# Cross-attention and mixture-of-experts block on one core: turning the attention output in 32x32 blocks on VectorE instead of on TensorE, with the low parts of x, context and attention output on GpSimd

## The reference

```python
x = x + xattn(layernorm(x), ctx)         # 16 heads of 16, softmax over 128 context tokens, then wo and its bias
x = x + ffn(layernorm(x))                # top-1 of 8 experts; LayerNorm again inside, scale/bias per expert,
                                         # 256 -> 64, exact gelu, 64 -> 256, only the chosen expert's row is kept
```

## Time and profile before

| what | value |
|---|---|
| time, median of 3 runs | 1593.97 us (1592.43 to 1604.42) |
| the profiled execution's own time | 1596.52 us |
| its span (first to last instruction) | 1594.5 us |
| busy PE / DVE / ACT / POOL | 94% / 75% / 56% / 27% of the span |
| attention | the first 1056 us or so |
| chain of work that ended last | PE 89%, DVE 5%, issue 3%, ACT 2% |

### The profile page before, as it was taken

How to read it: one execution, slowest core, us unless ns; L and a number is a source line. 1 busy time by engine, 2 the same in 40 slices (tenths; PEclk the granted TensorE clock), 3 DMA queues, 4 the chain that set the end, 5 groups by cost and what they waited for, 6 DMA issues and landing times.

```text
span 1594.5 us, 39584 instructions
## 1 busy us (share of the span) xinstructions
PE 1506.3 (94%) x15438; PEld 1210.1 (76%) x15438; DVE 1188.9 (75%) x2880; ACT 891.7 (56%) x1450; POOL 424.2 (27%) x600
## 2 busy tenths in 40 slices
PE   6899999999999999999999999879999999999998
PEld 5677777777778777878877787757777777777776
DVE  4787788767887788778777877667777777777775
ACT  4567666666667667767776777543342423333332
POOL 3223222222223223222322232112323232222221
PEclk9999999999999999999999999999999999999999
DMA  7466545554566556645654665402221212121221
GB/s 185 120 174 164 156 126 154 150 152 135 141 161 160 153 137 162 170 135 154 162 155 133 157 167 145 117 30 70 66 68 54 80 54 80 54 80 54 70 64 40
DMA packets 150480, 190.89 MB, mean 120 GB/s; under 512 B 17631, under 2 KB 101146, under 8 KB 150298
## 3 DMA queue, kind: packets, MB, share of 16 engines
q1 hardware_dynamic: 150298, 188.38, 43.1%
HBM read 53.01 MB, written 33.55 MB: 54 GB/s over the span
## 4 chain that ended last, share of the span: by engine, by line
PE 89%; DVE 5%; issue 3%; ACT 2%; DMA 1%; SPq 0%; ACTq 0%
PE s_ps L1195 12%; PE st_ps L1213 12%; PE pp_ps L1075 11%; PE pv_ps L1023 9%; PE s_ps L980 8%; PE pp_ps L1048 7%; PE st_ps L1008 7%; PE pp_ps L1083 5%; PE pp_ps L1069 4%; PE pv_ps L1031 3%; PE t_ps L999 3%; DVE negmax L729 2%; PE pp_ps L1161 2%; PE s_ps L1202 2%; ACT pT L636 1%
## 5 line engine op out<-in xcount | busy, mean ns | idle before, releaser
L729 DVE TENSOR_REDUCE negmax<-s_ps 128x8 f32<-128x1024 f32 x256 | 312.4, 1221 | 90.7 <-PE s_ps L980 83.4
L585 ACT ACTIVATE pT<-st_ps 128x1024 f32<-128x1024 f32 x256 | 262.7, 1026 | 101.9 <-PE st_ps L1008 101.8
L1213 PE MATMUL st_ps<-w_hi,q_packed 128*128 128x256 f32 x1024 | 213.2, 294 | 0.7 <-DVE q_packed L840 0.7
L1195 PE MATMUL s_ps<-k_packed,w_hi 128*128 128x512 f32 x512 | 172.8, 419 | 18.4 <-ACT pT L636 18.4
L1023 PE MATMUL pv_ps<-pT,v 128*32 128x128 f32 x4096 | 166.5, 278 | 24.8 <-DVE attn L742 12.5
L456 POOL TENSOR_TENSOR q_parts<-q,q_parts 128x1024 bf16<-128x1024 f32 x32 | 68.3, 2134 | 446.0 <-ACT q_parts L579 446.0
L980 PE MATMUL s_ps<-k_packed,q_packed 96*128 96x128 bf16 x2048 | 158.7, 221 | 18.4 <-issue 13.7
L1213 PEld LDWEIGHTS st_ps<-w_hi,q_packed 128*128 128x128 f32 x1024 | 168.4, 189 | 9.8 <-issue 6.4
L628 ACT ACTIVATE offhotT<-pv_ps 96x512 bf16<-96x512 bf16 x31 | 18.4, 592 | 253.1 <-PE pv_ps L1182 253.1
L1008 PE MATMUL st_ps<-q_packed,k_packed 98*128 98x128 bf16 x2048 | 158.9, 221 | 0.2 <-DMA q_packed<-negmaxT 0.2
L980 PEld LDWEIGHTS s_ps<-k_packed,q_packed 96*128 96x128 bf16 x2048 | 124.1, 98 | 44.3 <-issue 29.0
(11 more groups left out here) (179 smaller groups left out, 3511.7 us busy)
## 6 DMA issues: line engine op xcount, KB each, us to landing
q_packed<-q_parts SPq DMA_DIRECT2D x192, 256.0 KB, 3.8
k_packed<-k_parts SPq DMA_DIRECT2D x192, 256.0 KB, 4.4
xin<-in_x_dram SPq DMA_DIRECT2D x32, 512.0 KB, 3.8
cin<-in_ctx_dram SPq DMA_DIRECT2D x32, 512.0 KB, 3.9
x_scratch<-xb SPq DMA_DIRECT2D x32, 512.0 KB, 4.3
xin<-x_scratch SPq DMA_DIRECT2D x32, 512.0 KB, 4.6
out_dram<-xb SPq DMA_DIRECT2D x32, 512.0 KB, 3.2
q_packed<-negmaxT SPq DMA_DIRECT2D x128, 8.0 KB
```

What stands on the lines that cost most here:

```text
L585: a.activation(pT[u % 2][:], st_ps[:], ACT.Exp, scale=DH ** -0.5).then_inc(s_exp, 1)
L729: v.tensor_reduce(own, s_ps[:].rearrange("p (h s) -> p h s", s=P), AX_X, ALU.max, negate=True).then_inc(s_red, 1)
L1195: t.matmul(h_ps[m % 2], w[:, c, e, :].bitcast(F32R), x[n % 2][:, c, :].bitcast(F32R), start=(k == 0 and c == 0), stop=False)
L1213: t.matmul(o, h[n % 2][:, m, tok].bitcast(F32R), w[:, m, :].bitcast(F32R), start=(m == 0 and k == 0), stop=False)
```

## The change

DVE has an instruction that transposes each 32x32 block of its input by itself. As every head fills exactly 32 rows of `pv_ps`, one such instruction turns the bank into a tile with queries on the partitions, and a second one turns the divided result back for the projection. The order of features that this leaves is made good by a permuted order of wo's columns and v's bias. In detail:

- PE: `turn_pv` and `turn_attn` go; `values` of a new sequence waits for DVE's first turn (it waited for the division); `turn_max` waits for nothing of the attention output any more. Items 2 to 5 no longer wait for the low parts but for ACT; items 4 and 5 wait for the low parts of x, 6 and 7 for those of the context.
- ACT: `keep_pvT` goes; for items 0 to 3 it copies the bank a second time, in full precision, to the SBUF tile `turned[k % 2]`, once POOL has read what was there before. `keep_attn` reads SBUF.
- DVE: `turn_values` (a 128x512 transpose from PSUM) comes first in odd units, ahead of `maxima`; `norm` now ends with a 128x256 transpose in SBUF, which waits until ACT and POOL have read the sequence before; `rest_of_attn` and `lower` go.
- POOL: it takes `rest_of_attn` (128x256) and `lower` (128x512, from `turned`). Its group is no longer three calls but an order by pairs of units, and `residual` is cut in two halves.
- Start: POOL copies wo into the new order ahead of its first `norm`, once wo has been loaded; v's bias is loaded with two DMAs in runs of 16 numbers. The one-hot tiles of the expert layer lie in the same memory as `turned`.

```diff
@@ gpsimd
+            pool.wait_ge(s_w[3], 16)
+            for co in range(C):
+                for c in range(C):
+                    g.tensor_copy(wo_dense[:, co, c * P:(c + 1) * P].rearrange("p (s f d) -> p s f d", s=STRIPS, f=2),
+                                  dense(w_in[3][:, co, :])[:, c]).then_inc(s_wd, 1)
...
+            def rest_of_attn(n, b):
+                pool.wait_ge(s_ath, at(GB, n, b + 1))
+                hi, lo = aT[b % 2]
+                g.tensor_tensor(lo[:].bitcast(F32R), attnT[:], hi[:], ALU.subtract).then_inc(s_ate, 1)
+            def lower(n, k):
+                hi, lo = (xT, cT)[k // 2]
+                pool.wait_ge(s_pe, at(ITEMS, n, k + 1))
+                g.tensor_tensor(lo[:, k % 2, :].bitcast(F32R), turned[k % 2], hi[:, k % 2, :],
+                                ALU.subtract).then_inc(s_tl, 1)
...
-            def group(n):
-                if n < LAST:
-                    lo(n + 1, 0)
-                if n + 2 <= LAST:
-                    norm(n + 2)
-                if n < LAST:
-                    lo(n + 1, 1)
-                    residual(n + 1)
+            def group(n):
+                for u in range(0, UNITS, 2):
+                    if turned_at(n, u):
+                        rest_of_attn(*turned_at(n, u))
+                    if u == 0 and n < LAST:
+                        lo(n + 1, 0)
+                    if u == 2 and n + 2 <= LAST:
+                        norm(n + 2)
+                    if u == 2 and n < LAST:
+                        lo(n + 1, 1)
+                    if u == 4 and n + 2 <= LAST:
+                        lower(n + 2, 0)
+                    if u == 4 and n < LAST:
+                        residual(n + 1, 0)
+                    if u == 4 and n + 2 <= LAST:
+                        lower(n + 2, 1)
+                        lower(n + 2, 2)
+                    if u == 4 and n < LAST:
+                        residual(n + 1, 1)
+                    if u == 6 and n + 2 <= LAST:
+                        lower(n + 2, 3)
@@ scalar
-            def keep_pvT(n, b):
-                act.wait_ge(s_pv, at(UNITS, n, C * (b + 1)))
-                wait(act, s_tpv, at(GB, n, b))
-                a.copy(uvT[:], pv_ps[:]).then_inc(s_uv, 1)
...
-                    last = a.copy((xT, cT)[k // 2][0][:, k % 2, :].bitcast(F32R), ps[:])
+                    a.copy((xT, cT)[k // 2][0][:, k % 2, :].bitcast(F32R), ps[:]).then_inc(s_full, 1)
+                    wait(act, s_tl, at(4, n, k - 1))
+                    last = a.copy(turned[k % 2], ps[:])
@@ vector
+            def turn_values(n, b):
+                dve.wait_ge(s_pv, at(UNITS, n, C * (b + 1)))
+                wait(dve, s_nrm, at(GB, n, b))
+                v.transpose(pv_by_q[:], pv_ps[:]).then_inc(s_tpv, 1)
             def norm(n, b):
                 dve.wait_ge(s_tpv, at(GB, n, b + 1))
                 v.reciprocal(recip[:], pv[:, :, DH]).then_inc(s_rc, 1)
...
+                dve.wait_ge(s_nrm, at(GB, n, b + 1))
+                wait(dve, s_ath, at(GB, n, b))
+                wait(dve, s_ate, at(GB, n, b))
+                v.transpose(attnT[:].rearrange("p c t -> p (c t)"), attn[:]).then_inc(s_at, 1)
@@ tensor
                 if m == 0:
-                    wait(pe, s_nrm, at(GB, n, b))
+                    wait(pe, s_tpv, at(GB, n, b))
...
-            def turn_pv(n, b):
-                pe.wait_ge(s_uv, at(GB, n, b + 1))
-                for k in range(4):
-                    mm = t.transpose(pv_ps[:, k * P:(k + 1) * P], uvT[:, k * P:(k + 1) * P], ident[:])
-                mm.then_inc(s_tpv, 1)
...
-                if 2 <= k < 6:
-                    pe.wait_ge(s_tl, at(4, n, k - 1))
+                if 4 <= k < 8:
+                    pe.wait_ge(s_tl, at(4, n, 2 * (k // 2 - 1)))
```

More of the change, by code:

```diff
@@ L117, in xattn_moe @@
         v1 = [sb(f"v{n}", [P, GB, H, HP]) for n in range(2)]
+        shared = sb("shared", [P, 2, GT])
+        turned = [shared[:, n, :] for n in range(2)]
         xb = [sb(f"xb{n}", [P, GB, D]) for n in range(2)]
@@ L456, in lo, with residual @@
                 g.tensor_tensor(parts[z][:, 2, :, :], z32[z][:], parts[z][:, 1, :, :], ALU.subtract).then_inc(s_lo, 1)
[L458 to L463, removed]
+            def rest_of_attn(n, b):
[7 more added lines that the diff above has]
+                                ALU.subtract).then_inc(s_tl, 1)
+            def residual(n, half):
+                if half == 0:
+                    pool.wait_ge(s_xn, at(GB, n, GB))
+                    wait(pool, st_x2[n % 2], (n // 2) * 16)
+                for b in range(2 * half, 2 * half + 2):
                     last = g.tensor_tensor(xb[n % 2][:, b, :], xin[n % 2][:, b, :], bo_all[:], ALU.add)
-                last.then_inc(s_xb, 1)
+                if half == 1:
+                    last.then_inc(s_xb, 1)
             norm(0)
+            for k in range(4):
+                lower(0, k)
             g.memset(v1[0][:, :, :, DH:HP], 1.0).then_inc(s_vone, 1)
@@ L472, in _ @@
             g.memset(v1[1][:, :, :, DH:HP], 1.0).then_inc(s_vone, 1)
+            for k in range(4):
+                lower(1, k)
             pool.wait_ge(s_bo, 1)
-            residual(0)
+            for half in range(2):
+                residual(0, half)
             for e in range(E):
@@ L513, in lo_of_xT @@
                                 ALU.subtract).then_inc(f_xl, 1)
-            ffn_norm(0)
-            ffn_norm(1)
+            def group(n):
[19 more added lines that the diff above has]
+                        lower(n + 2, 3)
+                    if u == 2 and n == LAST:
+                        ffn_norm(0)
+                    if u == 4 and n == LAST:
+                        ffn_norm(1)
+            for n in range(GROUPS):
+                group(n)
             lo_of_xT(0)
+            rest_of_attn(LAST, GB - 2)
+            rest_of_attn(LAST, GB - 1)
             def ffn_group(n):
@@ L874, in _ @@
             v.tensor_copy(bo_all[:], t_ps[:, 0:D]).then_inc(s_bo, 1)
-            for k in range(3):
-                lower(1, k)
             dve.wait_ge(s_c1T, 1)
@@ L883, in _ @@
             last.then_inc(s_c1, 1)
-            lower(1, 3)
             remainder(1, 4)
@@ L900, in group @@
                         remainder(n + 2, 4)
-                    if more2 and u == 6:
-                        rest_of_attn(*done)
-                        lower(n + 2, 3)
-                    if more2 and u == 5:
-                        norm(*done)
+                    if done and u % 2 == 1:
+                        turn_values(*done)
                     if later(n, u, 3):
                         maxima(*later(n, u, 3))
-                    if done and u % 2 == 1 and not (more2 and u == 5):
+                    if done and u % 2 == 1:
                         norm(*done)
@@ L1236, in odd @@
             def odd(n, u):
-                ahead, nxt, done = later(n, u, 3), later(n, u, 1), turned_at(n, u)
+                ahead = later(n, u, 3)
                 if ahead:
```

97 lines of the change are left out of this document (34 added, 63 removed).

## The result

| kernel | median | runs |
|---|---|---|
| before | 1593.31 us | 1592.43 to 1604.42 (4) |
| after | 1655.71 us | 1654.19 to 1658.76 (4) |

The ratio is 1.0377 (95% interval 1.0329 to 1.0426): slower by 62 us, where 1586 was forecast and 1636 was the upper end of the range. The profiled execution has a span of 1654.4 us.

The account below looks back on a forecast made before the run. PE looked like the bound, but SP queue, POOL and DVE end the three stretches: 7.0 + 8.9 + 15.0 = 30.9 against 31.1 us, -6; start +4, end -6: -8, profiled 1588.5, median 1586 us; range 1548 to 1636.

Parts of the forecast that it names:

- four maxima at 1.56: DVE's four maxima in units 7, 0, 1 and 2, counted as 6.24 us of its 14.5 us sum.
- units 7, 0, 1 and 2: Stretch of a group, 15.60 us before: DVE will be last, 15.0 us after, gain 0.6 us.
- Units 3 and 4: Stretch of 7.18 us before: PE waits for the SP queue's last pack of k until about 7.0, gain 0.2 us.
- Units 5 and 6: Stretch of 8.32 us before: PE waits for POOL's low part of the attention output, 8.9 us, loss 0.6 us.
- Rival D: POOL is slowed by its neighbour DVE, one 0.42 us case a group in units 5 and 6: +12, 1598; chance 0.08.
- the transposes: DVE's new turns in odd units: 0.69 us for 128x512 and 0.41 for 128x256, 4.4 us a group.
- The start: Start of the kernel: POOL copies wo first, PE's first item moves from 13.01 to about 16.6: +4, between 0 and 8.
- The end: Last two groups: PE waits for the first turn alone, no longer for the division: -6, between -8 and 0.
- Rival A: In each group POOL and the pack do not hold PE; 29.3 us a group, about 1545 in all; chance 0.22.
- Rival B, the clock: Waits at unit 5 and in unit 6 lower the clock; half the groups lose about 1.7 us: +26, 1612; chance 0.15.
- a sign of being wrong: The forecast is wrong if the clock column falls below 0.97 in the steady windows.
- Rival C, slow turning: DVE's turns take their upper bounds, 1.6 us a group more in units 7 to 2: +50, 1636; chance 0.15.

Follow-up runs that it names:

- without the reads: The two small DVE instructions of the maxima made memsets that read nothing, in both kernels: after 1573.49 us, before 1579.19 us.
- with one input each: Kernel after, with the two small DVE instructions of the maxima replaced by three reductions that each read one SBUF tile: 1610.18 us, ratio 1.0089.
- the turning alone: Kernel before plus only the two DVE turns replacing PE's and ACT's copy; low parts stay on DVE, POOL keeps its old list: 1691.89 us, ratio 1.059.
- experiment 1: Both kernels with the small maxima instructions as memsets, maxima not subtracted from the scores: after 1573.49 us (ratio 0.9871), before 1579.19 us (0.9897).

## Why the prediction was wrong

By its own steps:

- **"four maxima at 1.56 (1.22 and two small ones, each after the one before)": the term that failed.** It stands in the sum for units 7, 0, 1 and 2, where DVE was rightly held to be last, and it priced L783 and L785 at their time in before. One of the eight there met POOL's `lo` of q in every group and waited for it, 1.83 us a group. The stretch was forecast at 15.0 and took 17.31 us in the mean. That it is this term: without the reads the stretch is 14.41, or 15.3 with the shorter `memset`s made good (eight times 0.106); with one input each it is 15.76, or 15.0 less the third instruction's four times 0.2. Some 0.2 to 0.5 us of the 17.31 is left to other causes, the clock among them.
- **The rest of the walk held.** Units 3 and 4: 7.71 against 7.77 before, a gain of 0.1 where 0.2 was forecast. (The 7.0 of the prediction is for the one group that it walked, which was shorter than the mean.) In the group shown above they took 8.35 us (676.80 to 685.15), with the last pack of k issued 2.52 us behind unit 3 as forecast. In the trace it landed at 685.06, 5.74 us later, where 4.4 were counted; such late landings are in before too (mean 4.85 us in both kernels). Units 5 and 6: 8.89 us for 8.9 forecast (8.43 before), with PE's wait of 1.10 for POOL's low part (692.94 above), behind exactly the queue that was walked. It is there with and without collisions, at 1.1 and 1.0 us.
- **Rival D had the right resource and the wrong victim.** It let POOL be slowed by the new division, at 0.42 us once a group. The instructions to count were the ones already there, 16 small ones a group with two inputs in SBUF, and it is mostly DVE that waits, for what is left of POOL's instruction. A collision costs up to the length of the other engine's instruction, not its own: that is why eight numbers could cost 2.14 us. With the trace's price, one collision of 1.83 us a group on DVE's part of the path, the forecast of 1586 becomes 1586 + 1.83 x 32 = 1645, against 1656 measured.
- **What the profile of before could have said.** L732 and L734 have a longest of 0.65 beside a median of 0.17 (above). The prediction looked at the maxima of POOL's rows and not at those of DVE's, and it took the small share of such cases for proof that contention is small. POOL was busy 57 of 200 us in a schedule where its long instructions fell between the small pairs. The change took POOL to 97 and moved the pairs, and it is the second that cost: the collision in units 7, 0, 1 and 2 is with an instruction that before had too, and the turning alone has it as well.
- **Right:** the transposes (0.709 and 0.445 for 0.69 and 0.41). The Trainium skill, "Vector Engine (DVE) Microarchitecture Reference", section 3.8, gives one element per cycle and lane. The trace agrees as far as two points can: 256 elements more take 0.264 us, that is 1.03 ns each, near one cycle of the 0.96 GHz that the prediction used, and some 0.18 us would be the fixed part (estimates, as one of the two reads PSUM and the other SBUF).
- **Not shown:** the net worth of the change without collisions. Measured -6 us for -8, but within the noise (experiment 1). By stretches the two kernels without the reads differ by -0.1, +0.7 and -0.8 us a group (forecast -0.2, +0.6 and -0.6), which has the right signs and sizes.
- **Start and end** were smaller than forecast. The start, forecast at +4: PE's first item moved from 13.0 to 15.7 (16.6 forecast), but by the first scores of the second group after without the reads was level with before without them (67.7 and 68.0). The end, forecast at -6: from the third last group's first scores to the last `values` it took 3.9 us less (98.1 for 102.0). With the reads, after was 1.8 us late at the first place and 0.5 us longer at the second.
- **Rival A** is out: in all 24 groups of after between 200 and 1000 us `scores` of unit 5 starts 0.1 us behind the landing of the last pack, and PE waits for POOL's low part 24 times. The pack was a limit before as well: so it was there in 18 of 25 groups.
- **Rival B, the clock,** is at most a small part. The windows fell to 0.95, 0.96 and 0.97, below the 0.97 that the prediction named as a sign of being wrong, and to 0.92 in the turning alone, where PE waits most; without the reads they are at 0.98 and 0.99. What the clock takes is most likely within the 0.2 to 0.5 us a group that the first point leaves open. How much a full clock would give back was not tried.
- **Two ends of the range do not follow from their sums.** A's is 1545 and not the 1548 of the range; C's 1.6 us in 29 groups is 46 us, which gives 1632 and not 1636. The 1656 measured lies outside either way.
- **Rival C, slow turning,** is out: the transposes have no long ones (445/445/447).

## What to carry to other kernels

Before giving GpSimd more work, or moving VectorE's, list every VectorE instruction with two tiles in SBUF as inputs, small ones above all, and look at the longest beside the median of each: each can last as long as whatever GpSimd instruction it meets. Then ask in which stretch they fall: of some four collisions a group here only the one where VectorE was last did the harm. Tiny ones on the critical path are the worst case; fold them into the instruction ahead of them (here the reduction wrote bfloat16 itself, worth 106 us in after and 32 in before), or give them one input. A schedule that has no collisions owes it to its phase, and any edit that shifts the phase can lose it without touching either engine's work.

## What the runs showed of the hardware

- In every collision shown, the engine that started second ended only behind the one that started first; POOL, where it was first, took no longer than its usual time. Mostly POOL is first, its instructions being longer, but the other order is in the trace of after as well:

```profile
102.37 0.69 DVE L826 TENSOR_TENSOR w_chunk<-w_chunk,ecols 128x512 f32<-128x512 f32 x1
102.53 1.65 POOL L488 TENSOR_TENSOR xT_lo<-shared,xT_hi 128x512 fp32r<-128x512 f32 x1 [1.15 <-ACT shared L603]
...
105.97 1.27 POOL L488 TENSOR_TENSOR xT_lo<-shared,xT_hi 128x512 fp32r<-128x512 f32 x1 [0.41 <-ACT shared L603]
105.98 1.54 DVE L800 TENSOR_TENSOR attn<-pv_by_q,recip 128x256 f32<-128x256 f32 x1
...
107.20 1.47 POOL L488 TENSOR_TENSOR cT_lo<-shared,cT_hi 128x512 fp32r<-128x512 f32 x1
```

  L488 at 102.53 takes 1.65 for its usual 1.27 and ends 1.12 us behind DVE's L826 (two tiles in SBUF), which ends at 103.06. At 105.98 the division meets L488 and ends 0.28 us behind it, 0.14 less than its own 0.42; the next L488 then ends 1.15 us behind the division. So each ends some 0.14 us sooner behind the other than it takes by itself (an estimate from these rows), and so do the small ones: 0.17 us by themselves, 0.03 us behind POOL's end. The Trainium skill states this rule in "SBUF — State Buffer", section "Who interferes with whom": "Issue order, not op shape, decides who blocks", and a DVE instruction with two SBUF inputs contends with a GpSimd one that reads SBUF. The trace agrees in both orders; the prediction cited another page, which names the contention alone.
- Reductions, transposes, reciprocals (one input) and a product of PSUM by SBUF never got longer beside POOL in the rows above. In the attention part of after the longest of each is within 0.02 us of its median (reduction 1.226 for 1.212, transposes 0.718 for 0.708 and 0.447 for 0.445, reciprocal 0.255 for 0.247).
- A maximum of a tile with itself (L783) waits as one of two inputs does (0.172 to 2.136 us).
- In the start of attention a copy of float32 within SBUF on DVE also got longer, L831 1.04 to 1.41 us for the 0.42 of the same cast before; it was not studied further.
